# Graph layers on one core: the first k stack issued by ACT, stacks ahead of the weight stores, two early projections in free banks, late weights split in pieces

## The chip, the cores and the metric

One core of a Trainium2 chip runs the kernel, in one program. The metric is the device time in microseconds, the median of several runs.

## The reference

Sixteen graphs, each with x (512 nodes by 512 features) and a sparse symmetric adj (512 by 512). Everything is float32. Cut to what matters:

```python
q, k, v = split_heads(x @ Wq.T), split_heads(x @ Wk.T), split_heads(x @ Wv.T)   # 16 heads of 32
a = einsum('bhnd,bhmd->bhnm', q, k) * D ** -0.5 + (adj + adj)[:, None]
p = softmax(a, -1)                       # rows that are all zero give 0
x = layernorm(x + (p @ v, heads joined) @ Wo.T)
top1 = argmax(x.mean(1) @ router_w + router_b)          # one of 4 experts per graph
out = adj @ (x @ expert_w[top1])
y = relu(batch norm of out, by expert over all of its graphs)
x = layernorm(x + y)
```

## The kernel before

The kernel is written by hand, one instruction stream per engine, and every wait is a semaphore wait in that stream. Graphs b = 0 to 15 go through one software pipeline. A graph has 16 **units** u (4 groups of 4 heads, times 4 row tiles of 128), a unit has 4 **turns** j, one per head; turn r = 4u + j, 64 turns a graph. Per turn:

- PE turns (transposes) the attention tile of turn r into `t_bank` (`pe_turn`), makes the **score** of turn r + 12 into `s_bank` (`pe_scores`, LEAD = 12), then some **chunks** of the projections and of the rest of the layer, as the list `TASKS` and the allowance `HALF_SLOTS` give them. At even units it multiplies the turned tiles with v (`pe_pv`).
- DVE makes the logits of r + 12 (score, adj and row minimum in one instruction, `dve_logits`), copies the turned tile of j = 3 to `pt` (`dve_turned`), and sums up POOL's folds of a unit (`dve_total`), two units ahead.
- POOL adds up each logit tile in three folds (`pool_slot`), in the order of the turns.
- ACT takes the exponential of r + 10 (`act_exp_step`, EXP_LEAD = 10), which waits for POOL's first fold of it, and copies the turned tiles of j = 0 to 2.
- SP issues the DMAs, in program order: a DMA stands behind every wait ahead of it.

The projections are three passes of float32r matmuls with high and low halves of both operands (`three_pass`; 4 chunks of 3 matmuls, 12 in all). A q or k projection of a head group leaves PSUM as two halves, the high one by ACT (`act_task`), the low one by DVE (`dve_task`), both into `qk_t`, which has one place for q and one for k. From there 16 DMAs of 32 partitions and 64 KB each lay it out head by head as `q_stack` or `k_stack` (`stack`), two buffers each, `g % 2`. So the next group's eviction waits until the 16 DMAs before it have landed (`wait_stacked`), and a group's first score waits until both of its stacks have.

The weights come as plain float32 and are split into halves on the chip (`dve_split_weights`: a cast and a subtraction over 128x2048). Wq, Wk and Wv are split at the start, into `sup`, `ot` and `slot_b`, and all are stored to DRAM, from where the w loads (`load_qk_w`) fetch one group at a time into `qk_w`. Five projections, `AHEAD` (q and k of groups 0 and 1, q of group 2), run ahead of graph 0, straight from `sup` and `ot`. The **late weights**, Wo and the four experts, are split by DVE behind units 1, 3, 5, 7 and 9 of graph 0 (`SPLIT_SLOTS`), all through one raw buffer (`x1`) and one split buffer (`sup`): load, split, store, load the next.

From graph 1 on no weight is split. `graphs` runs the units: three units of scores ahead (u = -3 to -1), graph 0, graph 1, graphs 2 to 14 (all alike), graph 15, a tail; then the batch norm and the last layer norm.

## Time and profile before

| | |
|---|---|
| median of 3 runs | 2518.1 us (2517.59 to 2522.15) |
| profiled execution | 2520.1 us, its span 2518.3 us |
| mean granted TensorE clock | 0.951 of full speed |
| busy share of the span | PE 89%, DVE 69%, ACT 63%, POOL 69% |
| DMA | 472.66 MB, mean 188 GB/s |

All times in the rows are microseconds from the start of the span. The shares are means over a start, sixteen graphs and a tail, which have different limits; what the change touches lies in the first 240 us, so these are read stretch by stretch. PE's clock has two levels, 1.2 and 2.4 GHz; a granted clock of 0.50 is the lower, 1.00 the higher.

### The profile page before, as it was taken

To read this page: it belongs to the slowest core of one execution; us is meant where nothing else is said; L and a number is where in the kernel's file an instruction comes from. 1 tells how busy PE (TensorE), PEld (TensorE's weight loads), DVE (VectorE), ACT (ScalarE), POOL (GpSimd) and SP (SyncE) were. 2 spreads that over 40 slices of the span, in tenths; PEclk is the share of its full clock that TensorE was granted. 3 is DMA by queue.
4 is the path that set the end of the run, shared out by engine and by line. 5 is a ranking of instruction groups with operands and counts; after the bars stand their busy time and mean duration, and the time that the engine had idled before them with its cause. 6 is when DMAs were issued, how large, how long until landed. Compare 5 with 4: busy or idle time off the path is not lost.

```text
span 2518.3 us, 48708 instructions
## 1 busy us (share of the span) xinstructions
PE 2233.9 (89%) x14496; PEld 1721.1 (68%) x14496; DVE 1739.8 (69%) x4498; ACT 1586.9 (63%) x3762; POOL 1746.6 (69%) x3196
## 2 busy tenths in 40 slices
PE   3678899998989999998989999898989999898864
PEld 2456677776767777676767777676767777676653
DVE  2476776767686776768586776767677676867558
ACT  0456666666666666666666666666666666665447
POOL 0578777777777777677777777777777777777324
PEclk7789999999999999999999999999999999999987
DMA  6487465564747456464747556474846556473877
GB/s 219 129 270 252 120 201 175 171 198 139 221 126 251 129 175 194 158 194 130 241 127 228 151 180 187 142 217 130 250 119 205 173 168 198 135 224 102 313 283 286
DMA packets 213189, 472.66 MB, mean 188 GB/s; under 512 B 40832, under 2 KB 49024, under 8 KB 206144
## 3 DMA queue, kind: packets, MB, share of 16 engines
q1 hardware_dynamic: 212928, 469.55, 60.1%
q8 instruction: 119, 1.95, 0.3%
q14 instruction: 142, 1.16, 0.2%
HBM read 270.16 MB, written 65.01 MB: 133 GB/s over the span
## 4 chain that ended last, share of the span: by engine, by line
PE 74%; DVE 10%; issue 5%; ACT 3%; SPq 3%; POOL 3%; DMA 1%; DVEq 0%; POOLq 0%; ACTq 0%
PE t_bank L377 15%; PE p_bank L281 13%; PE p_bank L282 13%; PE p_bank L283 13%; PE o_bank L396 9%; PE s_bank L360 8%; SPq L773 2%; DVE att L541 2%; DVE xt L609 1%; POOL fold L742 1%; DVE x L609 1%; PE o_bank L387 1%; ACT att L453 1%; POOL fold L744 1%; ACT pt L515 1%
## 5 line engine op out<-in xcount | busy, mean ns | idle before, releaser
L742 POOL TENSOR_TENSOR fold<-att 128x256 f32<-128x256 f32 x1024 | 766.1, 748 | 492.9 <-DVE nmax L541 406.5
L541 DVE CUSTOM_DVE_ANT_0 att<-s_bank,adj_t 128x512 f32<-128x512 f32 x1024 | 695.7, 683 | 383.5 <-PE s_bank L360 382.5
L453 ACT ACTIVATE att<-att,nmax 128x512 f32<-128x512 f32 x1024 | 738.7, 722 | 181.8 <-POOL fold L742 166.3
L515 ACT ACTIVATE pt<-t_bank 128x512 f32<-128x512 f32 x768 | 452.8, 597 | 399.5 <-PE o_bank L396 268.9
L377 PE MATMUL t_bank<-ident,att 128*128 128x128 f32 x4096 | 637.6, 279 | 20.7 <-ACT pt L515 11.0
L377 PEld LDWEIGHTS t_bank<-ident,att 128*128 128x128 f32 x4096 | 507.1, 143 | 208.0 <-issue 77.6
L360 PE MATMUL s_bank<-k_stack,q_stack 128*128 128x512 f32 x1024 | 502.0, 491 | 73.0 <-DVE nmax L541 72.5
L744 POOL TENSOR_TENSOR fold<-fold 128x128 f32<-128x128 f32 x1024 | 500.5, 489 | 80.3
L749 POOL TENSOR_TENSOR fold<-fold 128x64 f32<-128x64 f32 x1024 | 356.3, 348 | 80.2
L360 PEld LDWEIGHTS s_bank<-k_stack,q_stack 128*128 128x128 f32 x1024 | 200.1, 195 | 92.2 <-DVE nmax L541 89.7
L396 PE MATMUL o_bank<-pt,v 128*32 128x256 f32 x4096 | 250.2, 385 | 5.4 <-issue 4.5
L281 PE MATMUL p_bank<-xt,qk_w 128*128 128x512 f32 x492 | 205.2, 417 | 50.2 <-DVE xt L609 50.2
L282 PE MATMUL p_bank<-xt,qk_w 128*128 128x512 f32 x492 | 204.3, 415 | 0.0
L283 PE MATMUL p_bank<-xt,qk_w 128*128 128x512 f32 x492 | 203.5, 414 | 0.0
L453 ACT ACTIVATION_READ_ACCUMULATOR att<-att,nmax 128x1 f32 x1024 | 200.0, 195 | 0.0
L396 PEld LDWEIGHTS o_bank<-pt,v 128*32 128x32 f32 x4096 | 123.2, 110 | 93.1 <-issue 30.0
L550 DVE COPY pt<-t_bank 128x512 f32<-128x512 f32 x256 | 175.5, 685 | 0.4 <-PE t_bank L377 0.3
L281 PEld LDWEIGHTS p_bank<-xt,qk_w 128*128 128x128 f32 x492 | 99.6, 202 | 62.0 <-issue 54.6
L556 DVE TENSOR_REDUCE total<-fold 128x4 f32<-128x256 f32 x256 | 106.1, 414 | 22.0 <-POOL fold L749 22.0
L427 ACT ACTIVATE qk_t<-p_bank 128x512 fp32r<-128x512 f32 x128 | 76.0, 594 | 70.1 <-DMA q_stack<-qk_t 37.2
L281 PE MATMUL p_bank<-sup,slot_a 128*128 128x512 f32 x256 | 102.5, 400 | 14.5 <-issue 11.9
L283 PEld LDWEIGHTS p_bank<-xt,qk_w 128*128 128x128 f32 x492 | 98.7, 201 | 23.2
(359 smaller groups left out, 3659.2 us busy)
## 6 DMA issues: line engine op xcount, KB each, us to landing
q_stack<-qk_t SPq DMA_DIRECT2D x1024, 64.0 KB, 3.1
k_stack<-qk_t SPq DMA_DIRECT2D x1024, 64.0 KB, 2.0
qk_w<-qk_split SPq DMA_DIRECT2D x123, 512.0 KB, 4.8
slot_a<-expert_split SPq DMA_DIRECT2D x16, 2048.0 KB, 8.0
slot_b<-vo_split SPq DMA_DIRECT2D x15, 2048.0 KB, 8.2
slot_a<-vo_split SPq DMA_DIRECT2D x15, 2048.0 KB, 9.6
stage<-in_xT SPq DMA_DIRECT2D x16, 1024.0 KB, 5.6
adj_t<-in_adj SPq DMA_DIRECT2D x64, 256.0 KB, 7.5
```

Source lines behind the costliest of these rows:

```text
L281: eng.matmul(bank, lhs(0), rhs(0), start=(kt == 0), stop=False)
L282: eng.matmul(bank, lhs(0), rhs(1), start=False, stop=False)
L283: return eng.matmul(bank, lhs(1), rhs(0), start=False, stop=last)
L360: eng.matmul(s_bank[r % 2][:, :], q_stack[:, g % 2, j, t * P:(t + 1) * P], k_stack[:, g % 2, j, :], start=True, stop=True).then_inc(pe["sc ...
L377: mm = eng.transpose(t_bank[r % 2][:, m * P:(m + 1) * P], att[:, u % 4, j, m * P:(m + 1) * P], ident[:, :])
L396: mm = eng.matmul(bank[j * HD:(j + 1) * HD, 0:2 * P], v[:, m, head * HD:(head + 1) * HD], pt[:, j, m, :], start=(m == 0), stop=(m == NT - ...
L453: eng.activation(att[:, u % 4, j, :], att[:, u % 4, j, :], ACT.Exp, bias=nmax[:, u % 4, j:j + 1], scale=-1.0, accum_out=rsum[:, u % 4, j:j ...
L515: eng.activation(pt[:, j, :, (u % 2) * P:(u % 2 + 1) * P], t_bank[r % 2][:, :].rearrange("p (m n) -> p m n", m=NT), ACT.Copy).then_inc(act ...
L541: eng.tensor_tensor_reduce(out=att[:, u % 4, j, :], in0=s_bank[r % 2][:, :], in1=adj_t[:, t, :], scale=-2.0, scalar=3.0e38, op0=ALU.add, o ...
L742: eng.tensor_tensor(fold1[:, :], a[:, 0:256], a[:, 256:512], ALU.add).then_inc(pool_fold1, 1)
L744: eng.tensor_tensor(fold1[:, 0:P], fold1[:, 0:P], fold1[:, P:2 * P], ALU.add).then_inc(pool_halved, 1)
L749: eng.tensor_tensor(fold2[:, uu % 2, jj, :], fold1[:, 0:P // 2], fold1[:, P // 2:P], ALU.add).then_inc(pool_fold2, 1)
```

## The change

1. **K stack 0 from ACT.** The 16 DMAs of `stack(0, 1, 0)` go from SP's stream to ACT's, behind ACT's first two evictions.
2. **Order on SP.** The stacks of group 1 stand ahead of the eight stores of Wq and Wk and the store of Wv; before they stood behind them. The waits of ACT and DVE for these stores ahead of graph 0 are gone; those who overwrite the stored buffers wait there.
3. **Free banks.** The projections of q and k of group 1 go to `o_bank`, which nothing uses that early, instead of `p_bank`, so PE does not wait for an eviction; their evictions stand in units -3 of ACT and DVE. The fifth projection moves from ahead of the scores to behind score 8.
4. **Held weights.** K of group 2 and q of group 3 are projected straight from `ot` and `sup` (`HELD`), so two w loads fall away.
5. **Late weights in pieces.** Each late weight is split in four tiles of 128x512. ACT makes the high half of a piece at turns 0 and 2 of units 1, 2 and 4 to 11, DVE the low half one turn later. There are two raw buffers (`x1t`, `x1`) and two split buffers (`slot_a`, `sup`), used in turn. SP stores a finished weight behind units 2, 5, 7, 9 and 11 (`SPLIT_DONE`) and then issues the load that reuses its raw buffer. Weight n = 0 is Wo, n = 1 to 4 are experts 0 to 3.

In item 5 the loads are numbered as they stand: Wo is loaded at the start, expert 0 ahead of the weight stores, expert 1 behind unit 2, expert 2 behind unit 5, expert 3 behind unit 7.

```diff
@@ -49,7 +49,12 @@
-SPLIT_SLOTS = {1: 0, 3: 1, 5: 2, 7: 3, 9: 4}
+EARLY = 4
+HELD = (4, 3)
+SPLIT_AT = [(u, j) for u in (1, 2, 4, 5, 6, 7, 8, 9, 10, 11) for j in (0, 2)]
+SPLIT_HIGH = {(u, j): divmod(k, 4) for k, (u, j) in enumerate(SPLIT_AT)}
+SPLIT_LOW = {(u, j + 1): divmod(k, 4) for k, (u, j) in enumerate(SPLIT_AT)}
+SPLIT_DONE = {2: 0, 5: 1, 7: 2, 9: 3, 11: 4}
...
@@ -241,6 +248,8 @@
+            if b < 0 and task in AHEAD[2:EARLY]:
+                return o_bank[AHEAD.index(task) - 2]
             if b == B and task[0] in ("O-", "S-"):
...
@@ -297,14 +306,15 @@
                 g = i if not name.endswith("+") else GROUPS + i
-                if c == 0:
-                    first = sum(t[0] == ("Q+", "K+")[which] for t in AHEAD)
-                    wait(eng, (ld_qw, ld_kw)[which], b, GROUPS * 16, (g + 1 - first) * 16)
+                held = g + GROUPS * b < HELD[which]
+                if c == 0 and not held:
+                    wait(eng, (ld_qw, ld_kw)[which], b, GROUPS * 16, (g + 1 - HELD[which]) * 16)
                     if i == 0:
...
                         wait(eng, act_xt, b, DT, 2 * DT)
-                mm = three_pass(eng, bank[:, :], lambda h: qk_w[:, which, h, c, :], lambda h: xt[:, h, c, :],
-                                c, c == DT - 1)
+                mm = three_pass(eng, bank[:, :],
+                                lambda h: hilo_buf[which][:, h, c, g * P:(g + 1) * P] if held else qk_w[:, which, h, c, :],
+                                lambda h: xt[:, h, c, :], c, c == DT - 1)
             elif name == "V":
...
@@ -398,6 +408,21 @@
+        def pe_ahead(eng, task):
+
+            if task in AHEAD[EARLY:]:
+                s, per, more = done_by(-1, AHEAD[0])
+                wait(eng, s, -1, per, more)
+            which = "QK".index(task[0][0])
+            eng.wait_ge(dve_split, 2 * (which + 1))
+            eng.wait_ge(act_xt, DT)
+            eng.wait_ge(dve_xt, DT)
+            for c in range(DT):
+                mm = three_pass(eng, bank_at(-1, task)[:, :],
+                                lambda h: hilo_buf[which][:, h, c, task[1] * P:(task[1] + 1) * P],
+                                lambda h: xt[:, h, c, :], c, c == DT - 1)
+            mm.then_inc(pe[task[0][0]], 1)
+
         def pe_slot(eng, b, u, kind, kind_before):
...
@@ -517,6 +546,18 @@
                     act_exp_step(eng, b, e)
+                if isinstance(b, int) and b == 0 and (u, j) in SPLIT_HIGH:
+                    n, t = SPLIT_HIGH[u, j]
+                    if t == 0:
+                        eng.wait_ge(ld_late[n % 2], 16 * (n // 2 + 1))
+                        if n == 1:
+                            eng.wait_ge(st_split, 16 * 9)
+                            eng.wait_ge(pe["Q"], GROUPS)
+                        if n >= 2:
+                            eng.wait_ge(st_late[n % 2], 16 * (n // 2))
+                    eng.activation(split_late[n % 2][:, 0, t, :], raw_late[n % 2][:, t, :], ACT.Copy).then_inc(act_late, 1)
+                if isinstance(b, int) and b == 0 and (u, j) in AHEAD_AT:
+                    act_task(eng, -1, AHEAD_AT[u, j], FIRST)
                 for task, c in work[j]:
...
@@ -719,6 +760,13 @@
                         dve_low(eng, x1_lo_home(b)[:, t, :], x1_home(b)[:, t, :], x1t[:, t, :]).then_inc(dve_lo["X"], 1)
+                if isinstance(b, int) and b == 0 and (u, j) in SPLIT_LOW:
+                    n, t = SPLIT_LOW[u, j]
+                    eng.wait_ge(act_late, NT * n + t + 1)
+                    dve_low(eng, split_late[n % 2][:, 1, t, :], raw_late[n % 2][:, t, :],
+                            split_late[n % 2][:, 0, t, :]).then_inc(dve_late, 1)
+                if isinstance(b, int) and b == 0 and (u, j) in AHEAD_AT:
+                    dve_task(eng, -1, AHEAD_AT[u, j], FIRST)
                 for task, c in work[j]:
...
@@ -801,8 +849,12 @@
             if u == 2 and attends:
-                load_qk_w(eng, b, 1, 3)
+                if b > 0:
+                    load_qk_w(eng, b, 1, 3)
                 stack(eng, b, 1, 2)
+                if b == 0:
+                    eng.wait_ge(st_split, 16 * 9)
+                    load_qk_w(eng, b, 1, 3)
             if u == 4 and attends:
...
@@ -933,7 +985,14 @@
         sup_w = sup[:].bitcast(F32)
-        SPLIT_STORES = 4 + 4 + 1 + 1 + E
+        raw_late = [x1t_f[0], x1]
+        split_late = [slot_a, sup]
+        AHEAD_AT = {(-3, 0): AHEAD[2], (-3, 1): AHEAD[3], (-1, 0): AHEAD[4]}
+
+        def wait_late_stores(eng):
+
+            eng.wait_ge(st_late[0], 16 * 3)
+            eng.wait_ge(st_late[1], 16 * 2)
...
@@ -987,34 +1046,30 @@
             sp.wait_ge(ld_raw, 32)
-            sp.dma_start(x1[:, :, :], by_tile(wvT)).then_inc(ld_raw, 16)
+            sp.dma_start(x1, by_tile(wvT)).then_inc(ld_raw, 16)
             for t in range(NT):
                 sp.dma_start(adj_t[:, t, :], adj[0, t * P:(t + 1) * P, :]).then_inc(ld_adj[t], 16)
+            sp.dma_start(raw_late[0], late[0]).then_inc(ld_late[0], 16)
             stack(sp, 0, 0, 0)
-            stack(sp, 0, 1, 0)
+            stack(sp, 0, 0, 1)
+            stack(sp, 0, 1, 1)
+            sp.wait_ge(dve_split, 6)
+            sp.dma_start(raw_late[1], late[1]).then_inc(ld_late[1], 16)
             for which in range(2):
-                sp.wait_ge(dve_split, 2 * (which + 1))
                 for g in range(GROUPS):
...
                                  hilo_buf[which][:, :, :, g * P:(g + 1) * P].bitcast(F32)).then_inc(st_split, 16)
-            sp.wait_ge(dve_split, 6)
             sp.dma_start(vo_dram[0], slot_b[:].bitcast(F32)).then_inc(st_split, 16)
-            stack(sp, 0, 0, 1)
-            stack(sp, 0, 1, 1)
-            sp.wait_ge(st_split, 16 * 9)
-            load_qk_w(sp, 0, 1, 2)
-            load_qk_w(sp, 0, 0, 3)
...
-                if u in SPLIT_SLOTS:
-                    n = SPLIT_SLOTS[u]
-                    if n == 0:
-                        sp.dma_start(x1[:, :, :], late[0]).then_inc(ld_raw, 16)
-                    sp.wait_ge(dve_split, 6 + 2 * (n + 1))
-                    sp.dma_start(vo_dram[1] if n == 0 else ex_dram[n - 1], sup_w).then_inc(st_split, 16)
-                    if n + 1 < len(late):
-                        sp.dma_start(x1[:, :, :], late[n + 1]).then_inc(ld_raw, 16)
+                if u in SPLIT_DONE:
+                    n = SPLIT_DONE[u]
+                    sp.wait_ge(dve_late, NT * (n + 1))
+                    sp.dma_start(vo_dram[1] if n == 0 else ex_dram[n - 1],
+                                 split_late[n % 2][:].bitcast(F32)).then_inc(st_late[n % 2], 16)
+                    if n + 2 < len(late):
+                        sp.dma_start(raw_late[n % 2], late[n + 2]).then_inc(ld_late[n % 2], 16)
             graphs(sp, sp_slot, in_first=late_weights)
...
@@ -1074,9 +1129,9 @@
             act.activation(xt[:, 0, :, :], stage[:, :, :], ACT.Copy).then_inc(act_xt, DT)
-            for task in AHEAD:
+            for task in AHEAD[:2]:
                 act_task(act, -1, task, FIRST)
-            act.wait_ge(st_split, 16 * 9)
+            stack(act, 0, 1, 0)
             graphs(act, act_slot)
...
@@ -1123,19 +1178,9 @@
             dve_split_weights(dve, x1[:, :, :], slot_b[:].bitcast(F32), 2)
-            for task in AHEAD[2:]:
-                dve_task(dve, -1, task, FIRST)
-            dve.wait_ge(st_split, 16 * 9)
             dve.wait_ge(pool_const, 4 + E)
             dve.wait_ge(ld_const, 16)
-
-            def late_weights(u):
-                if u in SPLIT_SLOTS:
-                    n = SPLIT_SLOTS[u]
-                    dve.wait_ge(ld_raw, 16 * (3 + n + 1))
-                    dve.wait_ge(st_split, 16 * (9 + n))
-                    dve_split_weights(dve, x1[:, :, :], sup_w, 3 + n)
-            graphs(dve, dve_slot, in_first=late_weights)
+            graphs(dve, dve_slot)
```

Three places, as the streams are written. On ACT, from its first instruction of graph 0's preparation to the exponentials; `qk_t<-...` are the evictions, L453 (L480 after) the exponentials. Before:

```order
L1076 ACTIVATE xt<-stage 128x2048
L427 ACTIVATE qk_t<-p_bank 128x512 [waits pe_Q]
L427 ACTIVATE qk_t<-p_bank 128x512 [waits pe_K]
L427 ACTIVATE qk_t<-p_bank 128x512 [waits q_stacked0,pe_Q]
L427 ACTIVATE qk_t<-p_bank 128x512 [waits k_stacked0,pe_K]
L427 ACTIVATE qk_t<-p_bank 128x512 [waits q_stacked1,pe_Q]
L453 ACTIVATE att,rsum<-att,nmax 128x512 [waits pool_fold1,dve_logit,st_split]
```

And of the change:

```order
L1131 ACTIVATE xt<-stage 128x2048
L454 ACTIVATE qk_t<-p_bank 128x512 [waits pe_Q]
L454 ACTIVATE qk_t<-p_bank 128x512 [waits pe_K]
L821 DMA k_stack<-qk_t 32x512 [waits dve_lo_K,act_hi_K]
L821 DMA k_stack<-qk_t 32x512 x15
L454 ACTIVATE qk_t<-o_bank 128x512 [waits q_stacked0,pe_Q]
L454 ACTIVATE qk_t<-o_bank 128x512 [waits k_stacked0,pe_K]
L480 ACTIVATE att,rsum<-att,nmax 128x512 [waits pool_fold1,dve_logit] x7
L454 ACTIVATE qk_t<-p_bank 128x512 [waits q_stacked1,pe_Q]
```

The 16 DMAs came in, and the last eviction, which waits for q stack 1, moved behind seven exponentials.

On SP, from the first stack to the first late weights. Before:

```order
L773 DMA q_stack<-qk_t 32x512 x16
L773 DMA k_stack<-qk_t 32x512 x16
L998 DMA qk_split<-sup 1024x1x128 x4
L998 DMA qk_split<-ot 1024x1x128 x4
L1001 DMA vo_split<-slot_b 128x4096
L773 DMA q_stack<-qk_t 32x512 x16
L773 DMA k_stack<-qk_t 32x512 x16
L779 DMA qk_w<-qk_split 128x1024 x2
L773 DMA q_stack<-qk_t 32x512 x16
L1013 DMA x_0<-in_woT 128x4x512
```

And of the change:

```order
L821 DMA q_stack<-qk_t 32x512 x32
L821 DMA k_stack<-qk_t 32x512 x16
L1057 DMA x_0<-in_experts 128x4x512
L1060 DMA qk_split<-sup 1024x1x128 x4
L1060 DMA qk_split<-ot 1024x1x128 x4
L1062 DMA vo_split<-slot_b 128x4096
L821 DMA q_stack<-qk_t 32x512 x16
L821 DMA k_stack<-qk_t 32x512 x16
L827 DMA qk_w<-qk_split 128x1024
L1069 DMA vo_split<-slot_a 128x4096
L1072 DMA x1t<-in_experts 128x4x512
L848 DMA stage<-in_xT 128x4x512
```

The stores moved from between the stacks of groups 0 and 1 to between those of groups 1 and 2.

Further on SP in graph 0, from the fourth q stack (units 4 to 8), of the change:

```order
L821 DMA q_stack<-qk_t 32x512 x16
L827 DMA qk_w<-qk_split 128x1024
L821 DMA k_stack<-qk_t 32x512 x16
L1069 DMA expert_split<-sup 128x4096
L1072 DMA x_0<-in_experts 128x4x512
L827 DMA qk_w<-qk_split 128x1024
```

The store of expert 0 and the load of expert 2 (L1069, L1072) stand behind both stacks of group 3.

## Rows read from the trace of the kernel before

**Rows 1.** Busy time by stretch: start:end, length, each engine, clock, DMA share, GB/s
```profile
20.00:41.40 21.40, 10.65 (x35) 7.74 (x33) 5.50 (x5) 1.55 (x3) 0.00 (x0) 0.76 0.38 92
49.60:72.20 22.60, 0.68 (x3) 0.24 (x1) 0.54 (x1) 0.60 (x1) 0.00 (x0) 0.58 0.78 246
...
92.60:239.60 147.00, 119.66 (x764) 86.40 (x763) 99.20 (x227) 92.71 (x220) 112.56 (x202) 0.89 0.76 240
239.60:382.70 143.10, 134.17 (x892) 103.80 (x891) 101.93 (x270) 93.98 (x225) 107.50 (x200) 0.98 0.57 174
617.20:760.30 143.10, 134.47 (x892) 103.95 (x891) 101.77 (x268) 94.02 (x224) 106.15 (x197) 0.98 0.59 178
```

**Rows 2.** Timeline of ACT, 18 to 75 us: start, duration, instruction, idle before
```profile
22.51 0.60 ACT L427 ACTIVATE qk_t<-p_bank 128x512 fp32r<-128x512 f32 x1 [2.15 <-PE p_bank L283]
...
42.93 0.60 ACT L427 ACTIVATE qk_t<-p_bank 128x512 fp32r<-128x512 f32 x1 [9.53 <-DMA k_stack<-qk_t]
71.03 0.60 ACT L427 ACTIVATE qk_t<-p_bank 128x512 fp32r<-128x512 f32 x1 [27.51 <-DMA q_stack<-qk_t]
```

**Rows 3.** Timeline of DVE: the first logit
```profile
72.27 0.68 DVE L541 CUSTOM_DVE_ANT_0 att<-s_bank,adj_t 128x512 f32<-128x512 f32 x1
```

**Rows 4.** Timeline of SP's queue, 0 to 110 us: issue start, time of the issues
```profile
21.17 10.11 SPq L773 DMA_DIRECT2D q_stack<-qk_t  x16
31.38 10.03 SPq L773 DMA_DIRECT2D k_stack<-qk_t  x16
41.45 4.26 SPq L998 DMA_DIRECT2D qk_split<-sup  x4
...
55.24 14.26 SPq L773 DMA_DIRECT2D q_stack<-qk_t  x16
69.61 10.36 SPq L773 DMA_DIRECT2D k_stack<-qk_t  x16
```

**Rows 5.** Timeline of POOL: the first folds of two scores
```profile
73.04 0.73 POOL L742 TENSOR_TENSOR fold<-att 128x256 f32<-128x256 f32 x1 [71.36 <-DVE nmax L541]
...
74.86 0.73 POOL L742 TENSOR_TENSOR fold<-att 128x256 f32<-128x256 f32 x1
```

**Rows 6.** Timeline of PE: a k projection's first and last matmul, thirteenth score
```profile
34.17 0.79 PE L281 MATMUL p_bank<-xt,ot 128*128 128x512 f32 x1 [8.98 <-DVE qk_t L610]
...
39.03 0.60 PE L283 MATMUL p_bank<-xt,ot 128*128 128x512 f32 x1
...
88.46 0.80 PE L360 MATMUL s_bank<-k_stack,q_stack 128*128 128x512 f32 x1 [3.36 <-DVE nmax L541]
```

**Rows 7.** Timeline of DVE: one turned copy per unit; units 0, 12, 14, next graph's 0
```profile
98.38 0.69 DVE L550 COPY pt<-t_bank 128x512 f32<-128x512 f32 x1
...
208.71 0.69 DVE L550 COPY pt<-t_bank 128x512 f32<-128x512 f32 x1
...
223.48 0.69 DVE L550 COPY pt<-t_bank 128x512 f32<-128x512 f32 x1
...
239.69 0.69 DVE L550 COPY pt<-t_bank 128x512 f32<-128x512 f32 x1
```

**Rows 8.** Groups by line, ACT and DVE, 92 to 240 us
```profile
L941 DVE TENSOR_TENSOR sup<-x,sup 128x2048 fp32r<-128x2048 f32 x5 | 12.4, 2486 | 0.2
...
L939 DVE CAST sup<-x 128x2048 fp32r<-128x2048 f32 x5 | 6.2, 1237 | 10.5 <-DMA x<-in_woT 5.9 <-DMA x<-in_experts 4.6
...
L609 DVE TENSOR_TENSOR xt<-stage,xt 128x512 fp32r<-128x512 f32 x4 | 3.5, 874 | 0.0
...
L504 ACT ACTIVATE xt<-stage 128x512 fp32r<-128x512 f32 x4 | 2.5, 620 | 0.0
```

**Rows 9.** Timeline, 174 to 186 us: a store, the load behind it, who waits
```profile
174.05 0.34 SPq L1015 DMA_DIRECT2D expert_split<-sup  x1
174.43 0.44 SPq L1017 DMA_DIRECT2D x<-in_experts  x1
...
185.64 1.23 DVE L939 CAST sup<-x 128x2048 fp32r<-128x2048 f32 x1 [0.75 <-DMA x<-in_experts]
```

More of the change, by code:

```diff
@@ L1219, in _ @@
             eng.wait_ge(ld_const, 16)
-            for n, task in enumerate(AHEAD):
-                earlier = [t for t in AHEAD[:n] if bank_of[t] == bank_of[task]]
-                if earlier:
-                    s, per, more = done_by(-1, earlier[-1])
-                    wait(eng, s, -1, per, more)
-                which = "QK".index(task[0][0])
-                eng.wait_ge(dve_split, 2 * (which + 1))
-                eng.wait_ge(act_xt, DT)
-                eng.wait_ge(dve_xt, DT)
-                for c in range(DT):
-                    mm = three_pass(eng, p_bank[bank_of[task]][:, :],
-                                    lambda h: hilo_buf[which][:, h, c, task[1] * P:(task[1] + 1) * P],
-                                    lambda h: xt[:, h, c, :], c, c == DT - 1)
-                mm.then_inc(pe[task[0][0]], 1)
+            for task in AHEAD[:EARLY]:
+                pe_ahead(eng, task)
             graphs(eng, pe_slot)
```

10 lines of the change are left out of this document (8 added, 2 removed).

## The prediction, made before the change was run

> **What bounds the kernel now.** I read the busy time by stretch first. From graph 1 on the kernel repeats itself: 239.6 to 382.7 us and 617.2 to 760.3 us are both 143.1 us long, with PE busy 134 of them [rows 1]. The change touches nothing there, so its whole worth is how much earlier graph 1 begins. My mark is the turned copy of its unit 0, at 239.69 us in the profile of before [rows 7]; whatever moves that copy moves the end.
>
> Ahead of that lie two stretches that are not PE's. From 49.6 to 72.2 us nothing computes: PE 0.68 us busy, DVE 0.54, POOL none [rows 1]. The timeline of ACT names the cause: its eviction of q group 2 waits 27.51 us, to 71.03, for the stack of q group 1, and the first logit of DVE stands behind it at 72.27 [rows 2, 3]. SP's queue says why that stack is late: it is issued from 55.24, behind the weight stores begun at 41.45, which are behind the first k stack, which is behind the first q stack [rows 4]. Then graph 0 runs. Its last units take 14.77 us for eight turns, 208.71 to 223.48 [rows 7], 1.85 us each, which is POOL's own pace: two folds begin 1.82 us apart even with nothing else to do [rows 5]. But turn 3 to turn 67, 98.38 to 239.69, take 141.3 us where 64 turns at 1.85 are 118. The rest is mostly DVE splitting the five late weights whole: 12.4 + 6.2 us busy and 10.5 us idle for loads [rows 8], during which no logit is made.
>
> **The start, step by step.** Up to the low half of k group 0 all is as before: ACT evicts at 22.51 to 23.11, DVE needs 0.7 more, 23.8.
> - K stack 0. Its 16 issues now begin on ACT at 23.9 while SP's q stack runs from 21.17. No trace row has a DMA issued by ACT. The nearest rows are SP's own, 10.11 and 10.03 us for 16 [rows 4]; from below the cost is nothing, from above ACT's issues go only when SP's are done, which is before's time. I take SP's cost: issued by 34.0, landed 1.5 later (before: 41.41 issued, ACT released at 42.93 [rows 2, 4]), so 35.5.
> - First logit. Score 0 follows at 35.5 and the first logit at 36.4, against 72.27. ACT is held by its issues until 34.0, which costs nothing but the eviction of q group 1: nobody needs ACT earlier. That eviction, then its low half behind logit 0 on DVE, ends at 37.7.
> - Stacks of group 1, on SP: 37.8, then 10.1 and 10.1 for k: issued by 58.0, landed 59.5. They are needed for score 16, about 7 us after turn 0.
> - POOL starts at 37.2 and takes a score per 1.82 us: four by 44.5 (DVE's total of unit 0 waits for these), eight by 51.8, twelve by 59.0.
> - The fifth projection now stands on PE behind score 8. Score 8 comes at 45.3, the projection takes 5.5 us at the low clock (34.17 to 39.63 for a like one [rows 6]), so 51, its two halves end at 52.4, and the logit behind them is in time for POOL at 53.6. Price if late: what is over.
> - Scores 9 to 11 and turn 0 follow; score 12, the first beside V's chunks, comes at about 54.6 where it came at 88.46 [rows 6]. **The start gains 34 us**, and the copy of turn 3 moves from 98.38 to 64.5.
>
> The Trainium skill speaks against the first of these steps: its page "DMA: Bandwidth & Descriptors", section "Issuing engines are not separate DMA queues", says that DMAs begun on several engines run on the same 16 DMA engines and save only the sequencer's time, usually small beside the DMA itself. Here the rows show the reverse ratio: 16 issues take 10.1 us and the last one has landed 1.5 us later. By that rule taken strictly the k stack would land at before's 42.9 and the sum be some 7 us less, which is a rival below.
>
> **Graph 0, step by step.** The split itself gets cheap: 40 pieces of 128x512 instead of ten instructions of 128x2048. The 20 on ACT cost about 0.6 us each by a like piece (0.62), the 20 on DVE 0.7 to 0.87 (the x pieces, mean 0.874) [rows 8]; DVE's 18.6 busy us become 14 to 17, ACT gains 12 in a stretch where it is busy 92.7 of 147 us [rows 1]. Spread one per two turns beside 1.85 us a turn, they hide under POOL. What can wait is their data, and that hangs on SP's queue:
> - after 58.0: a load, 0.5; the weight stores, 13.8 as before (41.45 to 55.24); 72.3. Nobody waits for them now but the pieces of expert 0 and the w loads.
> - q stack 2: 14.3 behind those stores (55.24 to 69.50 before), 86.5; k stack 2: 10.4, 96.9, landed 98.4 [rows 4]. It is needed for score 32. POOL reaches fold 32 at about 99 (fold 12 at 59, twenty at 1.85, and PE's slower V units, some 3): even, at most 2 us late.
> - a w load, the store of the first piece set, the load of expert 1, xT and another w load: five issues of about 0.5 (0.34 and 0.44 in [rows 9]), 99.6.
> - q stack 3, crowded by 3.5 MB just issued: 12, between 10.1 and 14.3; 111.6. k stack 3: 11 with its w load; 122.6. Both are in time (score 48 comes after 125).
> - only then the store of expert 0 and the load of expert 2, which share expert 0's buffer pair. Such a store and load took from 174.05 until DVE got its data at 185.64, 11.6 us [rows 9]; so the data is there at 134.3.
> - the pieces of expert 2 begin in unit 8, which POOL's pace would reach at about 123 to 125. ACT stands 10 us at its first piece, DVE at the first low half behind it, and logits 46 on are not made. POOL has three more to do, so it starves from about 128 to 136.5: **8 to 9 us lost**.
> - From fold 46 at 136.5 POOL's pace holds (expert 3's load is issued at 125 and landed before unit 10 at 150). The exponential runs ten turns ahead of the turned copy (EXP_LEAD), so turn 67 goes with fold 77: 31 x 1.85 = 57.4, and 1.4 for the last unit (239.69 − 223.48 is 16.2, not 14.8). The mark comes at 195.3.
>
> Other waits: the first piece of expert 0 waits for the fourth q projection, which PE ends two turns later, some 2 us of ACT, hidden as POOL is two to four scores ahead; with that cover gone, 2 us. The pieces of expert 1 wait for a store issued at 98, there at 110 by the same 11.6 us, when POOL is not yet out of logits.
>
> **Sum.** 239.7 − 195.3 = 44.4 us: 34 at the start and 10 in graph 0. The profiled execution took 2520.1 us (span 2518.3); the median of the runs is 2518.1, 2 us below it. I take the gain from the median: 2474.
>
> **Rivals.**
> - No late wait reaches POOL. Then turn 67 is 64.5 + 118.4 + 1.4 + 3 = 187.3: gain 52, **2466**. For it: the buffers are doubled and only one wait is long by my sum. Against: a single stack more behind the stores moves it. 0.17.
> - ACT's issues do not run beside SP's: k stack 0 lands at 42.9, all later steps 7.4 later, **2481**. For it: the page above, and no row with two queues. Against: the DMA share was 0.38 from 20 to 41.4 us, where the two stacks went one after the other [rows 1], so two at once fit. 0.15.
> - The late waits are worse: the pieces of experts 1 and 3 starve POOL as those of expert 2 do, 8 us each, **2490**. For it: stores, loads and stacks share a queue whose DMA share was already 0.76 over graph 0 [rows 1], and now they are denser. 0.18.
> - Slower: every reload of experts 1 to 3 goes round fully in series, pieces (14.8 us for eight turns), two stacks (20.8), store and load (11.6), 47 us instead of 14.8 per two units, three times over: 97 us lost against the 52 of the ideal, **2563**. It decides as soon as more than one and a half of the three rounds are serial. Against: there are two buffers, and in unit 6 and 10 the load was issued before the stacks. 0.04.
> - No effect: the start's 34 us would have to come back as another wait and graph 0 take its 141 us again, **2518**. No step of the sum has room for it. 0.01.
>
> **The numbers.** Forecast 0.45, its own range 2468 to 2480. With the first three rivals the range is 2460 to 2491; it leaves out the last two and the worse half of the third, less than 0.2. A measurement of this kernel tells about 0.2%, 5 us: faster 0.95, same 0.01, slower 0.04.
>
> **What would show it.** In the profile after: first logit at about 36; the k stack's 16 issues on ACT from 23.9 for 10 us; score 12 near 54.6; the stores from 58.6; ACT waiting some 10 us for the load of expert 2 near 124 to 134, and no wait above 2 us at the pieces of expert 1 and 3; the turned copy of graph 1's unit 0 near 195; 143.1 us per graph behind it. Wrong would make me: ACT's issues much slower than 0.63 us each, weight stores that hold the second stacks longer than 14 us, or a steady graph that is no longer 143.1.

## The result, and the profile after

| | before | after |
|---|---|---|
| median of the runs | 2519.1 us (2517.6 to 2522.2) | 2483.7 us (2483.0 to 2485.4) |
| profiled execution, span | 2518.3 us | 2481.3 us |
| turned copy of graph 0, unit 0 | 98.38 [rows 7] | 61.99 |
| turned copy of graph 1, unit 0 | 239.69 [rows 7] | 204.88 |
| between the two | 141.3 | 142.9 |

After is faster: the ratio is 0.9861 (95% interval 0.9845 to 0.9876), 35.4 us. The forecast was 2474, 44 us faster; 2483.7 lies in its range (2460 to 2491), but above the likeliest case's own (2468 to 2480). The table already says where the difference lies: the start gave 36.4 us, and graph 0 took 1.6 us longer than before.

**The start.** The timeline of ACT after shows the first k stack on ACT's own queue (ACTq), 16 DMAs in 10.25 us. ACT was held 11.17 us while it issued them (third row), and then waited 0.77 us for them to land, in the fourth row; before it stood 9.53 us for this stack, and 27.51 us for the q stack of group 1 [rows 2].
```profile
23.11 0.60 ACT L454 ACTIVATE qk_t<-p_bank 128x512 fp32r<-128x512 f32 x1 [2.22 <-PE p_bank L292]
24.52 10.25 ACTq L821 DMA_DIRECT2D k_stack<-qk_t  x16
34.87 0.60 ACT L454 ACTIVATE qk_t<-o_bank 128x512 fp32r<-128x512 f32 x1 [11.17 <-issue]
36.24 0.60 ACT L454 ACTIVATE qk_t<-o_bank 128x512 fp32r<-128x512 f32 x1 [0.77 <-DMA k_stack<-qk_t]
```
SP's queue in the same profile (start of the issues, time of the issues). The first row holds q stacks 0 and 1 together. The weight stores at L1060 and L1062 now stand behind group 1's stacks, where they began at 41.45 [rows 4].
```profile
21.70 27.00 SPq L821 DMA_DIRECT2D q_stack<-qk_t  x32
48.80 10.04 SPq L821 DMA_DIRECT2D k_stack<-qk_t  x16
58.89 0.58 SPq L1057 DMA_DIRECT2D x<-in_experts  x1
59.51 7.55 SPq L1060 DMA_DIRECT2D qk_split<-sup  x4
67.10 6.21 SPq L1060 DMA_DIRECT2D qk_split<-ot  x4
73.37 1.55 SPq L1062 DMA_DIRECT2D vo_split<-slot_b  x1
75.05 14.50 SPq L821 DMA_DIRECT2D q_stack<-qk_t  x16
89.66 10.01 SPq L821 DMA_DIRECT2D k_stack<-qk_t  x16
...
101.37 1.69 SPq L848 DMA_DIRECT2D stage<-in_xT  x1
...
104.50 13.50 SPq L821 DMA_DIRECT2D q_stack<-qk_t  x16
...
118.73 10.01 SPq L821 DMA_DIRECT2D k_stack<-qk_t  x16
128.79 0.58 SPq L1069 DMA_DIRECT2D expert_split<-sup  x1
129.41 0.46 SPq L1072 DMA_DIRECT2D x<-in_experts  x1
```
The timeline of DVE has the first logit 35 us earlier than in [rows 3]:
```profile
37.31 0.69 DVE L582 CUSTOM_DVE_ANT_0 att<-s_bank,adj_t 128x512 f32<-128x512 f32 x1 [9.42 <-PE s_bank L370]
```
DVE stands idle for 9.42 us ahead of it. The empty 22.6 us of [rows 1] (49.6 to 72.2) have nothing of their length left here.

**Graph 0.** POOL takes one score after the other, so the time of the first fold of a score ("fold 32" is that of score 32) tells how far the graph is. Its timeline at scores 0, 32, 36, 46 and 77:
```profile
38.10 0.73 POOL L790 TENSOR_TENSOR fold<-att 128x256 f32<-128x256 f32 x1 [36.41 <-DVE nmax L582]
...
102.75 0.73 POOL L790 TENSOR_TENSOR fold<-att 128x256 f32<-128x256 f32 x1 [2.77 <-DVE nmax L582]
...
118.36 0.73 POOL L790 TENSOR_TENSOR fold<-att 128x256 f32<-128x256 f32 x1 [5.30 <-DVE nmax L582]
...
144.07 0.73 POOL L790 TENSOR_TENSOR fold<-att 128x256 f32<-128x256 f32 x1 [3.91 <-DVE nmax L582]
...
203.18 0.73 POOL L790 TENSOR_TENSOR fold<-att 128x256 f32<-128x256 f32 x1
```
Each of the three waits in the middle has a late transfer behind it, as the timelines of PE and ACT show:
```profile
101.17 0.77 PE L370 MATMUL s_bank<-k_stack,q_stack 128*128 128x512 f32 x1 [5.25 <-issue]
...
116.31 0.63 ACT L533 ACTIVATE xt<-stage 128x512 fp32r<-128x512 f32 x1 [4.81 <-DMA stage<-in_xT]
...
140.08 0.63 ACT L558 ACTIVATE sup<-x 128x512 fp32r<-128x512 f32 x1 [2.75 <-DMA x<-in_experts]
```
The first is score 32. Its releaser reads "issue", so the row doesn't name what it waited for. The times point to k stack 2: its last issue ended at 99.67, and 1.5 us, the landing time that the prediction took from [rows 2, 4], lead to 101.17. The second is the load of graph 1's xT. The third is the one that the prediction put at 10 us.

Busy time by stretch (columns as in [rows 1]): the two stretches between fold 32, fold 46 and fold 77, and graph 1.
```profile
102.75:144.07 41.32, 30.92 (x180) 22.14 (x178) 26.35 (x58) 24.20 (x57) 24.50 (x43) 0.79 0.93 313
144.07:203.18 59.11, 51.03 (x343) 35.44 (x342) 43.95 (x112) 45.31 (x109) 49.44 (x94) 0.89 0.90 272
```
```profile
204.88:348.00 143.12, 134.75 (x892) 104.07 (x891) 101.61 (x268) 93.96 (x224) 107.22 (x199) 0.98 0.61 184
```
POOL is busy 24.50 of 41.32 us in the first and 49.44 of 59.11 in the second. Both have the DMA engines 0.9 busy, so it is not the share alone that makes the first long. The steady graph (the last row) is 143.1 us long as before.

These three waits are not three prices that add up. From 75.05 to 129.87 us SP's queue issues without a gap of more than 0.11 us, and it ends with the load of expert 2 (L1072). Its data let ACT go on at 140.08, and fold 46 follows 3.99 us later. Kernel 5 below takes the second wait away, and the data of expert 2 still come at 139.78.

### The profile page after: what moved, and what is told of

Its sections match the earlier page's. It is cut to its first block, busy times and chain, and to the rows that moved or that the text cites. A ratio compares the mean times of both kernels' runs of the same rounds, so it can differ in the third digit from the quotient of the medians.

```text
span 2481.3 us, 48733 instructions
## 1 busy us (share of the span) xinstructions
PE 2229.5 (90%) x14496; PEld 1720.3 (69%) x14496; DVE 1735.1 (70%) x4508; ACT 1594.5 (64%) x3782; POOL 1739.9 (70%) x3196
## 4 chain that ended last, share of the span: by engine, by line
PE 73%; DVE 13%; issue 5%; ACT 3%; POOL 3%; SPq 1%; DMA 1%; ACTq 0%; DVEq 0%; POOLq 0%
PE t_bank L387 15%; PE p_bank L290 13%; PE p_bank L291 13%; PE p_bank L292 13%; PE o_bank L406 9%; PE s_bank L370 8%; DVE att L582 2%; DVE xt L650 1%; DVE x L650 1%; POOL fold L790 1%; ACT att L480 1%; PE o_bank L397 1%; SPq L821 1%; ACT pt L544 1%; POOL fold L792 1%
## 5 line engine op out<-in xcount | busy, mean ns | idle before, releaser
L480 ACT ACTIVATE att<-att,nmax 128x512 f32<-128x512 f32 x1024 | 739.1, 723 | 158.1 <-POOL fold L790 143.3
L290 PE MATMUL p_bank<-xt,qk_w 128*128 128x512 f32 x484 | 201.9, 417 | 49.2 <-DVE xt L650 48.0
L291 PE MATMUL p_bank<-xt,qk_w 128*128 128x512 f32 x484 | 200.6, 414 | 0.0
L480 ACT ACTIVATION_READ_ACCUMULATOR att<-att,nmax 128x1 f32 x1024 | 200.4, 196 | 0.0
L292 PE MATMUL p_bank<-xt,qk_w 128*128 128x512 f32 x484 | 199.9, 413 | 0.0
L406 PEld LDWEIGHTS o_bank<-pt,v 128*32 128x32 f32 x4096 | 122.6, 110 | 95.3 <-issue 31.6
L290 PEld LDWEIGHTS p_bank<-xt,qk_w 128*128 128x128 f32 x484 | 98.0, 202 | 62.5 <-issue 55.1
L290 PE MATMUL p_bank<-sup,slot_a 128*128 128x512 f32 x256 | 102.8, 402 | 14.5 <-issue 11.9
L597 DVE TENSOR_REDUCE total<-fold 128x4 f32<-128x256 f32 x256 | 106.0, 414 | 12.5 <-POOL fold L797 12.3
L292 PEld LDWEIGHTS p_bank<-xt,qk_w 128*128 128x128 f32 x484 | 96.7, 200 | 22.8
L291 PEld LDWEIGHTS p_bank<-xt,qk_w 128*128 128x128 f32 x484 | 97.0, 200 | 21.9
```

The costliest lines, as they stand in the source:

```text
L290: eng.matmul(bank, lhs(0), rhs(0), start=(kt == 0), stop=False)
L291: eng.matmul(bank, lhs(0), rhs(1), start=False, stop=False)
L292: return eng.matmul(bank, lhs(1), rhs(0), start=False, stop=last)
L406: mm = eng.matmul(bank[j * HD:(j + 1) * HD, 0:2 * P], v[:, m, head * HD:(head + 1) * HD], pt[:, j, m, :], start=(m == 0), stop=(m == NT - ...
L480: eng.activation(att[:, u % 4, j, :], att[:, u % 4, j, :], ACT.Exp, bias=nmax[:, u % 4, j:j + 1], scale=-1.0, accum_out=rsum[:, u % 4, j:j ...
```

## The experiments

All kernels are changes of the one after. The marks are read from DVE's timeline: the first logit, the logit of score 32, and the turned copy of graph 1's unit 0.

Two cautions go with the table. The kernel before was timed again beside each group and took 2519.5 us beside kernels 1 to 4, 2519.9 beside 5 to 8 and 2521.3 beside 9 to 12, so a difference of 2 us between groups is none between kernels. And the marks are of one profiled execution each, which was the slowest of its four in kernels 6 and 7 (4.5 and 5.1 us above the median) and the fastest in kernels 8 and 10 (3.4 and 3.0 below).

| kernel | median (range), us | ratio to before (95%) | logit 0 | logit 32 | mark |
|---|---|---|---|---|---|
| before | 2519.1 (2517.6–2522.2) | | 72.27 | 139.99 | 239.69 |
| after | 2483.7 (2483.0–2485.4) | 0.9861 (0.9845–0.9876) | 37.31 | 101.98 | 204.88 |
| 1 k stack 0 on SP | 2491.4 (2490.7–2493.6) | 0.9890 (0.9873–0.9906) | 43.69 | 110.17 | 213.54 |
| 2 stores first | 2490.1 (2487.3–2491.3) | 0.9881 (0.9865–0.9898) | 41.29 | 114.31 | 209.06 |
| 3 no late weights | 2469.2 (2467.1–2470.1) | 0.9798 (0.9782–0.9814) | 36.26 | 100.36 | 190.66 |
| 4 pieces only | 2472.8 (2471.6–2474.0) | 0.9813 (0.9797–0.9830) | 36.37 | 100.52 | 193.22 |
| 5 xT early | 2482.5 (2480.0–2484.2) | 0.9849 (0.9832–0.9865) | 37.49 | 101.99 | 204.69 |
| 6 Wv store in gap | 2484.9 (2483.0–2489.4) | 0.9859 (0.9842–0.9875) | 41.05 | 106.74 | 207.23 |
| 7 both of these | 2482.3 (2480.7–2487.4) | 0.9849 (0.9833–0.9866) | 41.41 | 104.44 | 205.24 |
| 8 Wv, Wq in gap, xT early | 2480.7 (2477.3–2483.8) | 0.9849 (0.9833–0.9865) | 42.47 | 106.77 | 201.53 |
| 9 pieces later | 2489.0 (2487.9–2489.9) | 0.9870 (0.9855–0.9885) | 37.14 | 102.18 | 207.30 |
| 10 Wq stores later | 2482.5 (2479.5–2486.4) | 0.9849 (0.9836–0.9863) | 37.26 | 96.33 | 203.54 |
| 11 and stack 3 first | 2489.0 (2485.3–2489.2) | 0.9866 (0.9851–0.9881) | 36.73 | 97.10 | 209.27 |
| 12 split whole | 2484.6 (2483.2–2487.0) | 0.9856 (0.9841–0.9871) | 37.59 | 102.34 | 204.54 |

**1. K stack 0 back on SP's queue.**
```diff
             stack(sp, 0, 0, 0)
+            stack(sp, 0, 1, 0)
             stack(sp, 0, 0, 1)
...
-            stack(act, 0, 1, 0)
```


> The changed kernel with k stack 0 back on SP, between q stack 0 and q stack 1. Theory 1 (two queues run side by side): k stack 0 is issued from about 31.9 to 42 instead of 24.5 to 34.8, the first logit comes about 7 us later, near 44.5, and all that SP does behind it 10 us later, so the turned copy of graph 1's unit 0 comes 7 to 10 us after 204.9 and the time is 2491 to 2494 us. Rival (the issues of two engines take turns, or the time gained at the start is lost again in graph 0, which waits for SP and the DMA queue): 2484 us, within 2.

Measured 2491.4, 7.7 us over after. SP's queue shows the two stacks one behind the other again:
```profile
20.91 10.11 SPq L821 DMA_DIRECT2D q_stack<-qk_t  x16
31.12 10.03 SPq L821 DMA_DIRECT2D k_stack<-qk_t  x16
45.06 10.01 SPq L821 DMA_DIRECT2D q_stack<-qk_t  x16
```
The first logit comes 6.4 us later. So ACT's queue is worth this much, and the other 30 of the start's 36 come from the order on SP, the free banks and the later place of the fifth projection together. Kernel 2 takes back the order alone; the banks, the fifth projection and the held weights were not tested by themselves.

**2. Weight stores back ahead of group 1's stacks.**
```diff
             stack(sp, 0, 0, 0)
-            stack(sp, 0, 0, 1)
-            stack(sp, 0, 1, 1)
...
             for which in range(2):
+                sp.wait_ge(dve_split, 2 * (which + 1))
                 for g in range(GROUPS):
...
             sp.dma_start(vo_dram[0], slot_b[:].bitcast(F32)).then_inc(st_split, 16)
+            stack(sp, 0, 0, 1)
+            stack(sp, 0, 1, 1)
```


> The changed kernel with the nine weight stores back ahead of the stacks of group 1; all else as changed. Q stack 1 lands near 61 instead of 49, so the fifth projection's eviction and the turned copy of unit 0 come about 10 us later (72 instead of 62). Theory 1 (graph 0 is held in units 5 and 6 by SP's queue and the full DMA engines, not by its start): q and k stack 2 no longer stand behind the stores, k stack 2 lands near 101 as now, and the loss of 10 us is made up by there; time 2484 to 2488 us. Rival (graph 0 takes its 143 us from wherever it starts): 2493 us.

Measured 2490.1, 6.4 over after and between the two theories. The copy of unit 0 comes 11.5 us later (73.47), but the mark only 4.2: from logit 32 to the mark it takes 94.8 us where after takes 102.9. The first theory had the loss made up ahead of score 32; logit 32 is still 12.3 us behind, and what is made up lies behind it. SP's queue has free time here (q stack 2 is issued by 83.57, k stack 2 from 92.00), where after's has none. At the start, the copy of unit 0 is still 24.9 us earlier than before. So the order is worth 11.5 us there and 6.4 at the end.

**3. No late weights.** This kernel leaves out the late loads, the pieces and their stores, and reads the split Wv in place of Wo's and the experts' split weights.
```diff
-                if isinstance(b, int) and b == 0 and (u, j) in SPLIT_HIGH:
+                if False:
...
-            sp.dma_start(raw_late[0], late[0]).then_inc(ld_late[0], 16)
...
-                if u in SPLIT_DONE:
+                if False:
```


> Leaves out the late weights: no load, no piece and no store of Wo and the experts; where these would be read, the split Wv is. Everything else as changed. Theory 1 (their traffic fills the queue behind which k stack 2, xT and the w loads wait): graph 0 takes 125 to 128 us instead of 142.9, time 2466 to 2470 us. Rival (POOL, DVE and PE pace graph 0 anyway): no more than 5 us gained, 2479 us or above.

**4. Pieces only.** Here the pieces are made at their places, but only the first late weight is loaded and none is stored; the split Wv is read in place of all five.
```diff
                     if t == 0:
-                        eng.wait_ge(ld_late[n % 2], 16 * (n // 2 + 1))
+                        if n == 0:
+                            eng.wait_ge(ld_late[0], 16)
...
-                        if n >= 2:
-                            eng.wait_ge(st_late[n % 2], 16 * (n // 2))
```


> As the one before, but ACT and DVE do all 40 pieces, on what lies in the two raw buffers; the reloads and stores of the late weights are left out. Theory 1 (the pieces themselves hide under POOL): within 3 us of the kernel with no late weights at all, 2467 to 2472 us. Rival (the pieces and their order on ACT and DVE cost the time): within 3 us of the changed kernel, 2481 us or above.

Measured 2469.2 and 2472.8, the second a little over its 2467 to 2472; graph 0 takes 129.7 us in kernel 3, above its 125 to 128. So all the work on late weights costs 14.5 us: 3.6 of it the pieces (the ranges of the two kernels are apart, their intervals overlap), 10.9 their loads and stores. Busy time by stretch of pieces only, fold 32 to fold 46 and fold 46 to fold 77:
```profile
101.28:132.43 31.15, 27.05 (x178) 19.53 (x178) 25.01 (x58) 23.70 (x57) 24.96 (x43) 0.91 0.55 152
132.43:191.51 59.08, 49.88 (x341) 35.02 (x342) 43.90 (x112) 45.37 (x109) 49.41 (x93) 0.91 0.62 193
```
Against after, the second stretch is equal to 0.03 us although after moves 272 GB/s there and this kernel 193. The first is 10.2 us shorter with the same POOL work. So nearly all that the late transfers cost (the two marks are 11.7 us apart) lies between scores 32 and 46. In the no-late kernel the timeline of PE still has this:
```profile
99.56 0.76 PE L370 MATMUL s_bank<-k_stack,q_stack 128*128 128x512 f32 x1 [8.53 <-issue]
```
With pieces (kernel 4) that score starts at 99.10. So fold 32 comes at the same time whether pieces are made or not, 101.14 and 101.28; without them PE merely waits longer, 8.53 us for 3.12. Up to score 32 the pieces are hidden.

**5. xT of graph 1 loaded ahead of the late store.**
```diff
-            if u == 4 and has_next:
+            if u == 4 and has_next and not (isinstance(b, int) and b == 0):
...
                     load_qk_w(eng, b, 1, 3)
+                    eng.wait_ge(act_xt, DT)
+                    eng.wait_ge(dve_xt, DT)
+                    eng.dma_start(stage[:, :, :], xT[1]...).then_inc(ld_xt, 16)
```


> The changed kernel with the load of graph 1's xT moved on SP from unit 4 to unit 2, just ahead of the store of Wo. Theory (the load waits behind a 2 MB store and a 1 MB load on full DMA engines, and ACT stands 4.8 us for it at unit 6, with logits stopped for longer): 2 to 5 us faster than the changed kernel, 2479 to 2482 us. Rival (the engines are full from 101 to 118 us whatever the order, and another wait takes its place): 2484 us, within 1.5.

Measured 2482.5, not to be told from after. The wait for xT is gone, and ACT's list of waits shows a new one at expert 1 and a longer one at expert 2, 5.0 us where after has 2.75 (ACT, 54 to 215 us; total, times, longest):
```profile
ACT sup L558 <- DMA x<-in_experts: 5.0, 1, 5.0
...
ACT slot_a L558 <- DMA x1t<-in_experts: 1.8, 1, 1.8
```
ACT's timeline gives the time of that wait's end, and POOL's that of fold 46:
```profile
139.78 0.63 ACT L558 ACTIVATE sup<-x 128x512 fp32r<-128x512 f32 x1 [5.02 <-DMA x<-in_experts]
143.77 0.73 POOL L790 TENSOR_TENSOR fold<-att 128x256 f32<-128x256 f32 x1 [6.10 <-DVE nmax L582]
```
Fold 36 comes 3.7 us earlier than in after, fold 46 only 0.3. The longest wait was not the one that ended last: what sets fold 46 is when expert 2's data land. In all eight kernels with the experts' pieces where after has them (after, 1, 2 and 4 to 8) fold 46 stands 3.99 us behind the first piece of expert 2, and in all but kernel 4 that piece waits for its data.

**6. Wv's store (2 MB) in the gap between SP's q stacks 0 and 1.**
```diff
             stack(sp, 0, 0, 0)
+            sp.wait_ge(dve_split, 6)
+            sp.dma_start(vo_dram[0], slot_b[:].bitcast(F32)).then_inc(st_split, 16)
             stack(sp, 0, 0, 1)
```


> The changed kernel with the one 2 MB store of the split Wv moved from behind the other eight into the gap of SP between q stack 0 and q stack 1, 32 to 38 us, where the DMA share is 0.38. Theory (k stack 2 is late because both group 2 stacks stand behind 6 MB of stores): k stack 2 lands near 95.5 instead of 101, q stack 1 at most 1 us later, 3 to 6 us faster, 2478 to 2481 us. Rival (what is gained at unit 5 is lost at unit 6 and 8, where the late loads are awaited): 2483 us.

Measured 2484.9, above the 2478 to 2481 hoped for: the gap isn't free. From 32 to 38 us the DMA share is 0.35 in after and 1.01 here, with 385 GB/s for 83. The timeline of ACT shows its k stack, which the store now runs beside:
```profile
23.95 12.99 ACTq L821 DMA_DIRECT2D k_stack<-qk_t  x16
37.05 0.60 ACT L454 ACTIVATE qk_t<-o_bank 128x512 fp32r<-128x512 f32 x1 [13.91 <-issue]
39.98 0.60 ACT L454 ACTIVATE qk_t<-o_bank 128x512 fp32r<-128x512 f32 x1 [2.33 <-DMA k_stack<-qk_t]
```
The issues take 12.99 in place of 10.25 us and are awaited 2.33 more; the first logit comes 3.7 us later. K stack 2 is now awaited 0.9 us, not 5.25, but expert 2's data land at 142.35, after a wait of 5.3 us, and fold 46 comes at 146.34. What is gained at unit 5 is gone at unit 8, as the rival had it.

**7. Both of these.** The edits of 5 and 6 in one kernel.

> Both moves of the two kernels before together. Theory (two waits in a row, each real): the gains add, 6 to 10 us faster than the changed kernel, 2474 to 2478 us. Rival (one queue, one total): no more than the better of the two alone.

Measured 2482.3: not to be told from either alone. ACT waits 5.5 us for expert 1 (to 118.45) and 2.8 for expert 2 (to 140.36), and fold 46 comes at 144.35.

**8. Wv's and Wq's stores in the gap, xT early.** As 7, with
```diff
+            for g in range(GROUPS):
+                sp.dma_start(qk_dram[0, g],
+                             hilo_buf[0]...).then_inc(st_split, 16)
             stack(sp, 0, 0, 1)
```


> As the kernel before, with the four stores of Wq in the gap too, 4 MB in all. Theory: q stack 1 stands behind them, lands 3 to 5 us later (near 53) and holds up the fifth projection's eviction by 2 to 4 us, but k stack 2 lands near 92, before PE asks for it; 2472 to 2476 us. Rival (the start costs more than k stack 2 gives): 1 to 4 us slower than the kernel before.

Measured 2480.7, the lowest of the full kernels, but 3.0 under after with intervals that overlap, and above the 2472 to 2476 hoped for. The start is 5.2 us later, and k stack 2, issued 4 us earlier (85.69 to 96.80), is awaited by nobody; expert 2's data land at 136.73, 3.4 us earlier than in after, fold 46 comes at 140.72, and logit 32 to mark takes 94.8 us.

**9. Pieces of the experts two units later.**
```diff
-SPLIT_AT = [(u, j) for u in (1, 2, 4, 5, 6, 7, 8, 9, 10, 11) for j in (0, 2)]
+SPLIT_AT = [(u, j) for u in (1, 2, 6, 7, 8, 9, 10, 11, 12, 13) for j in (0, 2)]
...
-SPLIT_DONE = {2: 0, 5: 1, 7: 2, 9: 3, 11: 4}
+SPLIT_DONE = {2: 0, 7: 1, 9: 2, 11: 3, 13: 4}
```


> The changed kernel with the pieces of experts 0 to 3 two units later (units 6 to 13, stores behind units 7, 9, 11, 13). Theory (late traffic in units 4 to 8 costs 11 us because it meets the stacks of group 3, xT and the w loads): the waits for late loads at units 6 and 8 go, xT's may stay; 2 to 5 us faster than the changed kernel, 2479 to 2482 us. Rival (same bytes, same loss, only later: the store of expert 3 and the loads of Wo meet graph 1's start): 2483 us or above.

Measured 2489.0, above the 2479 to 2482 hoped for. It is 5.3 us over after by the medians, but the before beside it took 2.2 us more, and the intervals of the ratios overlap. Fold 46 comes at 140.85, 3.2 us earlier than in after, and the mark 2.4 us later. The pieces wait for what their own last round of store and load brings, so asking later moves that round, too: ACT stands 5.2 us at expert 3 in unit 12.

**10. Wq's stores behind k stack 2.** With the edits of 5 and 9; the waits on the weight stores are split to match.
```diff
-            for which in range(2):
-                for g in range(GROUPS):
-                    sp.dma_start(qk_dram[which, g], ...
+            for g in range(GROUPS):
+                sp.dma_start(qk_dram[1, g], ...
...
                     load_qk_w(eng, b, 1, 3)
...
+                    for g in range(GROUPS):
+                        eng.dma_start(qk_dram[0, g], ...
```


> As the kernel before, and the four Wq stores behind k stack 2, with xT ahead of them; the w load of q group 4 waits for them ahead of q stack 3. Theory: with 2 MB and four issues of 1.9 us less in front, q stack 2 starts near 68.5 and k stack 2 lands near 93, before PE asks for it at 96; the 5 us of unit 5 go without any loss at the start (turned copy of unit 0 at 62). 5 to 9 us faster than the changed kernel, 2475 to 2479 us. Rival (the stores only move the queue: q stack 3 then comes too late): 2482 us or above.

Measured 2482.5, where the rival had put it. Logit 32 comes 5.6 us earlier than after, as meant; but from there to the mark it takes 107.2 us: PE waits 4.1 us for w (`qk_w<-qk_split`), ACT 2.9 for the buffer that Wq's stores still read and 7.3 for expert 3.

**11. Q stack 3 ahead of that w load.** As 10, with
```diff
+                    stack(eng, b, 0, 3)
+                    eng.wait_ge(st_split, 16 * 9)
                     load_qk_w(eng, b, 0, 4)
```


> As the kernel before, with q stack 3 ahead of the w load of q group 4, so that SP does not wait for the Wq stores. Theory: SP's wait of some 5 to 8 us ahead of q stack 3 goes; equal to the kernel before if q and k stack 3 were in time there, up to 4 us faster if not; 2473 to 2479 us.

Measured 2489.0, above its 2473 to 2479; its ratio's interval overlaps with after's, but its mark comes 4.4 us later. PE's timeline shows what the w load behind the stack costs:
```profile
127.13 0.77 PE L290 MATMUL p_bank<-xt,qk_w 128*128 128x512 f32 x1 [12.40 <-DMA qk_w<-qk_split]
```

**12. DVE splits each late weight whole.** The order of after on the queues, but the split as before: two instructions on DVE for each weight, where after has eight pieces on ACT and DVE.
```diff
-                if isinstance(b, int) and b == 0 and (u, j) in SPLIT_HIGH:
+                if False:
...
+                if isinstance(b, int) and b == 0 and u in SPLIT_DONE and j == 3:
+                    n = SPLIT_DONE[u]
...
+                    eng.tensor_copy(split_late[n % 2][:, 0], raw_late[n % 2]).then_inc(act_late, 1)
+                    eng.wait_ge(act_late, n + 1)
+                    dve_low(eng, split_late[n % 2][:, 1], raw_late[n % 2], split_late[n % 2][:, 0]).then_inc(dve_late, NT)
```


> The changed kernel, but DVE splits each late weight whole (a cast and a subtraction over 128x2048, behind units 2, 5, 7, 9 and 11) and ACT makes no piece; the same loads, stores, buffers and waits. Theory (pieces hide, blocks of 3.7 us on DVE stop the logits): 4 to 10 us slower than the changed kernel, 2488 to 2494 us. Rival (the data's arrival sets the pace, not who splits it): 2484 us, within 2.

Measured 2484.6, 0.9 over after with overlapping intervals, as the rival had it; the mark comes at 204.54. But the equal time hides two differences that cancel. Expert 2 is now asked for at the end of unit 9, not at the start of unit 8, so nobody waits for it, and fold 46 comes at 140.54, 3.5 us earlier than in after. From there to fold 77 it takes 62.3 us where after takes 59.1, and POOL doesn't stand idle in them: it is busy 53.0 us for 49.4. Its folds beside a whole split take longer, as the timelines of POOL and DVE show:
```profile
147.49 1.19 POOL L804 TENSOR_TENSOR fold<-fold 128x64 f32<-128x64 f32 x1
148.82 2.65 POOL L797 TENSOR_TENSOR fold<-att 128x256 f32<-128x256 f32 x1
```
```profile
147.01 1.48 DVE L771 CAST sup<-x 128x2048 fp32r<-128x2048 f32 x1
148.60 2.29 DVE L650 TENSOR_TENSOR sup<-x,sup 128x2048 fp32r<-128x2048 f32 x1
```
The like folds take 0.32 and 0.73 us elsewhere. So the pieces are worth 3.2 us in this stretch; that the total is equal comes from the later demand for expert 2.

## Why the prediction was right, and which step was off

- **The start, 34 us: right.** Measured 36.4 by the copy of unit 0. The k stack's issues took 10.25 us on ACT (SP's rate was taken, 10.1), ended at 34.77 for 34.0; first logit 37.31 for 36.4; the first score beside V's chunks at 54.63 for 54.6. The sum put the copy of turn 3 at 64.5 and it came at 61.99: what stands between score 12 and turn 3 was taken some 2.5 us too long.
- **The rival that ACT's issues don't run beside SP's: refuted.** SP's q stack 0 takes 10.15 us beside them in after (21.70 to 31.85, with ACT's from 24.52) and took 10.11 alone [rows 4], and kernel 1 puts the price at 7.7 us against the 7 that the prediction gave. The Trainium skill ("DMA: Bandwidth & Descriptors", "Issuing engines are not separate DMA queues") holds that a second issuer saves only the sequencer's time, usually small. Here that was nearly all the time of a stack, so the rule's mechanism stands and its "small" doesn't. Kernel 6 agrees with what the page also says, that all issuers run on the same DMA engines: a 2 MB store begun by SP makes ACT's stack some 4 us later.
- **Graph 0, 10 us: this step failed.** It took 142.9 us, not 130.8; as the start came out 2.5 us better, the mark is 9.6 us late, 204.88 for 195.3. The path was the one of the prediction: SP's queue down to expert 2's load, and fold 46 behind it. What was wrong is the length of that queue, and two terms behind it, as the table and the four points below it show:

| | forecast | measured | late so far |
|---|---|---|---|
| stacks of group 1 issued | 58.0 | 58.84 | 0.8 |
| a load and the weight stores, up to q stack 2 | 72.3 | 75.05 | 2.8 |
| k stack 2 issued | 96.9 | 99.67 | 2.8 |
| five single issues, up to q stack 3 | 99.6 | 104.50 | 4.9 |
| q stack 3 issued | 111.6 | 118.00 | 6.4 |
| k stack 3 issued | 122.6 | 128.74 | 6.1 |
| expert 2's data | 134.3 | 140.08 | 5.8 |
| fold 46 | 136.5 | 144.07 | 7.6 |
| mark | 195.3 | 204.88 | 9.6 |

- The queue, 5.8 us: the weight stores took 15.5 us (59.51 to 75.05), not 13.8; the "five issues of about 0.5" took 4.7 (99.77 to 104.50), 1.69 of them for xT's load and 1.29 for a w load; q stack 3 took 13.5, not 12.
- Up to fold 46, 1.8 us more: it stands 3.99 us behind the first piece of expert 2, where the prediction left 2.2.
- Behind it, 2.0 us: fold 46 to 77 had 57.4 us and took 59.1, and the last stretch 0.3 more. The pieces account for the 1.7: without them (kernel 3) the 31 turns take 56.6 us, 1.83 each; with them 59.1, 1.91 each, in after and in kernel 4 alike.
- The prediction also had ACT stand 10 us at expert 2 and nowhere else for more than 2 us. ACT stood 2.75 us there, because it came some 13 us later itself: k stack 2 ("even, at most 2 us late") held PE for 5.25 us and POOL for 2.77, and xT, which the prediction had only as an issue, held ACT for 4.81. Kernel 5 shows that the second of these waits is no loss of its own. That the first is none either is not shown by itself; in kernel 6, whose start is 3.7 us later, it shrinks to 0.9 us, and fold 46 still stands where expert 2's data put it.
- **How much of this is luck.** The range held because the rivals widened it. The measured 2483.7 is 9.7 us above the sum, and nearest to the rival of 2481, whose cause the runs refute.
- **Why it gained nothing against before.** Before lost time to whole splits and to loads behind them [rows 8]; after lost it to SP's queue, at the end of which expert 2's data come. From logit 0 to logit 32 after is 3.0 us shorter (64.7 for 67.7), from logit 32 to the mark 3.2 longer (102.9 for 99.7). Both store the five late weights in graph 0, and after has the weight stores there besides: between the two copies of unit 0 it moves 274 GB/s for 250. With the waits on late transfers gone (kernel 4) graph 0 takes 132.2 us, and with all or two thirds of the weight stores ahead of it (kernels 2 and 8) 135.6 and 134.4.
- **The other rivals.** "No late wait reaches POOL" fell: POOL stood idle 3.91 us behind expert 2's data. "The late waits are worse" was right that the queue would be the limit, wrong on where: neither expert 1 nor 3 was awaited. "No effect" said that graph 0 would take its 141 us again; it did, but the start's gain stayed. "Slower" fell with the time: no round of store and load held ACT for more than 2.75 us.
- **Open.** The mark moved by 34.8 us, the last turned copy of the whole kernel (2367.47 and 2330.50) by 37.0. The traces show where the 2.2 us lie: up to graph 15's unit 0 the difference is 35.3 (2244.46 and 2209.19), so 1.7 of them lie in graph 15. They may be nothing: from the mark to the end of the span the fourteen profiles take 2274.0 to 2280.6 us. Why stores take 14 to 15.5 us was not measured by itself. What the free banks, the place of the fifth projection and the held weights are worth singly stays open, too.
